# One transformer block with ternary weights: two soft thresholds, summed on TensorE, in place of compare and combine, and new queue orders

## What is computed

```python
def _bitlinear(x, w_latent):
    scale = clip(mean(abs(w_latent), axis=1), 1e-05, None)
    tern = clip(round(w_latent / scale), -1.0, 1.0)
    return x @ (tern * scale).T          # in value
...
h = _bitlinear(x, w_fc) + gate * (x @ v.T @ fast_b.T @ u.T)
r = maximum(h, 0.0)
return _bitlinear(r * r, w_proj)
```

## Time and profile before

| | us |
|---|---|
| median of 3 runs (lowest, highest) | 76.26 (76.23, 77.61) |
| the profiled execution's own time | 76.25 |
| span of its trace | 74.2 |
| busy in the span: PE, DVE, ACT, POOL | 65.0, 52.1, 39.7, 40.2 |

### The profile page before, as it was taken

How to read it: one execution, slowest core, us unless ns; L and a number is a source line. 1 busy time by engine, 2 the same in 40 slices (tenths; PEclk the granted TensorE clock), 3 DMA queues, 4 the chain that set the end, 5 groups by cost and what they waited for, 6 DMA issues and landing times.

```text
span 74.2 us, 2187 instructions
## 1 busy us (share of the span) xinstructions
PE 65.0 (88%) x902; PEld 57.6 (78%) x902; DVE 52.1 (70%) x106; ACT 39.7 (54%) x82; POOL 40.2 (54%) x46
## 2 busy tenths in 40 slices
PE   4999999999999869986678799749999999999950
PEld 3787888889987859974566577449899989999940
DVE  0000049760899999999999999999598344999850
ACT  6100005646794788920059991391739989769000
POOL 7300327891482999999999990000381999800000
PEclk9999999999999999999965559999999999999999
DMA  0999999999300000000000000000000000000044
GB/s 10 297 247 325 372 399 343 390 395 390 117 0 9 0 0 0 4 0 9 9 0 0 0 0 9 0 4 0 9 0 0 0 0 0 9 0 0 0 141 141
DMA packets 3497, 6.74 MB, mean 91 GB/s; under 512 B 528, under 2 KB 1296, under 8 KB 3488
## 3 DMA queue, kind: packets, MB, share of 16 engines
q1 hardware_dynamic: 3488, 6.60, 25.4%
HBM read 6.08 MB, written 0.52 MB: 89 GB/s over the span
## 4 chain that ended last, share of the span: by engine, by line
PE 54%; DVE 39%; issue 3%; ACT 1%
PE psum L312 14%; PE psum L465 10%; PE psum L496 10%; DVE fc_tern L770 7%; PE psum L505 4%; DVE prob_n L856 4%; DVE prob_t L861 3%; PE psum L475 3%; PE psum L414 3%; DVE fc_tern L765 2%; PE psum L407 2%; PE psum L332 2%; DVE k_spread L830 2%; DVE shifted L842 2%; DVE fc_sum L751 2%
## 5 line engine op out<-in xcount | busy, mean ns | idle before, releaser
L602 ACT ACTIVATE std<-mv,eps_sb 128x1 f32<-128x1 f32 x8 | 2.3, 293 | 13.8 <-DVE mv L786 13.8
L1023 POOL TENSOR_TENSOR kqv_sb<-head_sb 128x512 f32<-128x512 f32 x4 | 4.2, 1039 | 10.2 <-ACT head_sb L725 10.2
L782 DVE TENSOR_TENSOR h<-psum,pos_sb 128x256 f32<-128x256 f32 x4 | 1.6, 412 | 9.5 <-PE psum L312 9.5
L725 ACT ACTIVATE head_sb<-psum,fc_scale 128x256 f32<-128x256 f32 x16 | 6.7, 468 | 2.7 <-PE psum L475 2.7
L465 PE MATMUL psum<-zt_hi,fc_t 128*128 128x256 f32 x32 | 8.0, 284 | 0.0
L465 PE MATMUL psum<-zt_lo,fc_t 128*128 128x256 f32 x32 | 7.8, 279 | 0.0
L496 PE MATMUL psum<-sq_hi,mlp_t 128*128 128x256 f32 x32 | 7.8, 282 | 0.0
L496 PE MATMUL psum<-sq_lo,mlp_t 128*128 128x256 f32 x32 | 7.7, 279 | 0.0
L312 PE MATMUL psum<-head_sb 128*128 128x256 f32 x24 | 6.9, 456 | 0.0
L312 PEld LDWEIGHTS psum<-head_sb 128*128 128x128 f32 x24 | 5.5, 239 | 1.3 <-DMA head_sb<-head 0.3
L465 PEld LDWEIGHTS psum<-zt_lo,fc_t 128*128 128x128 f32 x32 | 6.0, 188 | 0.0
(11 more groups left out here) (123 smaller groups left out, 186.5 us busy)
## 6 DMA issues: line engine op xcount, KB each, us to landing
head_sb<-head SPq DMA_DIRECT2D x6, 256.0 KB, 4.9
fc_sb<-w_fc SPq DMA_DIRECT2D x2, 512.0 KB, 7.7
mlp_sb<-w_mlp SPq DMA_DIRECT2D x2, 512.0 KB, 9.1
tail_sb<-tail SPq DMA_DIRECT2D x2, 384.0 KB, 6.4
out_t<-tail_sb SPq DMA_DIRECT2D x4, 128.0 KB, 1.8
pos_sb<-pos SPq DMA_DIRECT2D x1, 256.0 KB, 5.4
kqv_sb<-w_k SPq DMA_DIRECT2D x1, 256.0 KB, 6.5
kqv_sb<-w_q SPq DMA_DIRECT2D x1, 256.0 KB, 6.6
```

Of the source, the lines that this page charges most:

```text
L725: nc.scalar.activation(part[:, a, :], FCB[n][:, a * HT:(a + 1) * HT], ACT.Relu, scale=fc_scale[:, 0, m:m + 1]).then_inc(relu_ready, 1)
L1023: pool.tensor_tensor(sq[:, r, :, :], relu[:, r, :, :], relu[:, r, :, :], ALU.mult).then_inc(sq_pool, 1)
```

## The change

1. **Two soft thresholds in place of compare and combine.** With s the scale, `over` = max(w, s/2) - s/2 and `under` = min(w, -s/2) + s/2 are each made by one instruction from w, independent of each other. PE turns both into the same place in PSUM (one product with the identity starts it, the second adds), and ACT takes the sign while copying out. The unders (8 of fc, 2 of mlp) and the over of the second mlp tile are POOL's, the fc overs DVE's (tiles 0, 1) and ACT's (tiles 2 to 7), the first mlp tile's over is ACT's. PE gets 32 products for fc where there were 16 and 32 for mlp where there were 16; ACT copies all four pieces, now of float32 where they were bfloat16.
2. **All fc sums on DVE**, in two pieces of four tiles.
3. **fast_b is folded into v** (`fold_v`, 2 products) and no longer into u (`fold_u`, 8 products); the transfers of u and v change places with it (u 64 KB late, v 17 KB early).
4. **New queue orders**: on PE `turn(1)` and `value(0)` stand ahead of `scores(0)`; `turn_fc` and `turn_mlp` stand around `project(0)`; `values(1)` and `project(1)` stand behind the first hidden products of half 0, which are split in the product with the rounded part and that with the remainder. `turn(1)` of layer norm 2 stands behind two `mlp_out`. On ACT the rectified tiles of half 1 go one ahead of the squares. Half 0's squares and remainders stay on POOL.

```diff
+        SQ_DVE, SQ_POOL = (4, 5, 6, 7), (0, 1, 2, 3)
...
-            def turn_mlp():
-                pe.wait_ge(mlp_ternary, KE)
...
+            def turn_mlp(i):
+                pe.wait_ge(mlp_over_act, 1)
+                pe.wait_ge(mlp_over_pool, 1)
+                pe.wait_ge(mlp_under_pool, KE)
+                for m in range(4):
+                    h = slice((4 * i + m) * P, (4 * i + m + 1) * P)
+                    for o in range(KE):
+                        c = (m % 2 * KE + o) * P
+                        for n, part in enumerate((mlp_over, mlp_under)):
+                            mm = pe.matmul(mlpt_ps[i][:, m // 2, c:c + P], part[:, o, h], ident_bf[:, :],
+                                           start=n == 0, stop=n == 1)
+                mm.then_inc(mlpt_turned, 1)
...
             turn_fc(0)
             pe.wait_ge(shift_ready, 2)
-            turn_u()
+            turn_fc(1)
             pe.wait_ge(duo_ready, 3)
-            turn_fc(1)
             project(0)
+            turn_mlp(0)
             pe.wait_ge(fct_ready, 1)
-            pe.wait_ge(ut_ready, 2)
-            pe.wait_ge(k_copied, 2)
+            turn_mlp(1)
+            pe.wait_ge(mlpt_ready, 1)
+            turn(0, z, z2t_ps[0], z2_ready, z2t_turned)
+            turn(0, h2, h2t_ps[0], h2_ready, h2t_turned)
+            hidden_main(0, 0, (z2t_hi,))
+            hidden_main(0, 1, (z2t_hi,))
+            low_rank(0)
+            hidden_main(0, 0, (z2t_lo,))
+            hidden_main(0, 1, (z2t_lo,))
+            hidden_low(0, 0)
+            pe.wait_ge(fct_ready, 2)
+            pe.wait_ge(mlpt_ready, 2)
             values(1)
...
+            def fc_signs(i):
+                act.wait_ge(fct_turned, i + 1)
+                nc.scalar.activation(fc_t[:, :, i * 512:(i + 1) * 512], fct_ps[i], ACT.Sign).then_inc(fct_ready, 1)
...
+            fc_signs(0)
             norm_std(0, 1, var2, std2)
+            mlp_signs(0)
             norm_std(1, 1, var2, std2)
+            fc_signs(1)
             copy_out(z2t_hi[0][:, :, :], z2t_ps[0][:, :], z2t_turned, 1, z2t_hi_ready)
-            duo_rows(1)
+            mlp_signs(1)
...
-            def fc_below(tiles):
+            def fc_overs(tiles):
                 dve.wait_ge(fc_scaled, 3)
                 for m in tiles:
-                    dve.tensor_scalar(fc_tern[:, m, :], fc_sb[:, m, :], fc_scale[:, 2, m:m + 1], None,
-                                      ALU.is_lt).then_inc(fc_cmp_dve, 1)
-
-            def ternary(w, scale, tern, m, cmp, count, ready):
-                dve.wait_ge(cmp, count)
-                dve.scalar_tensor_tensor(tern[:, m, :], w[:, m, :], scale[:, 1, m:m + 1], tern[:, m, :],
-                                         ALU.is_gt, ALU.subtract).then_inc(ready, 1)
...
-            def below(w, scale, dst, tiles, scaled, signal):
+            def unders(w, scale, dst, tiles, scaled, signal):
                 pool.wait_ge(scaled, 3)
                 for m in tiles:
-                    pool.tensor_scalar(dst[:, m, :], w[:, m, :], scale[:, 2, m:m + 1], None,
-                                       ALU.is_lt).then_inc(signal, 1)
+                    pool.tensor_scalar(dst[:, m, :], w[:, m, :], scale[:, 2, m:m + 1], scale[:, 1, m:m + 1],
+                                       ALU.min, ALU.add).then_inc(signal, 1)
```

More of the change, by code:

```diff
@@ L463, in hidden_main @@
                     for k in range(KE):
-                        for i, part in enumerate((z2t_hi, z2t_lo)):
-                            pe.matmul(FCB[n][:, a * HT:(a + 1) * HT], fc_t[:, k, m * P:(m + 1) * P],
-                                      part[f][:, k, :], start=a == 0 and k == 0 and i == 0, stop=False,
-                                      skip_group_check=True)
+                        for part in parts:
+                            pe.matmul(FCB[n][:, a * HT:(a + 1) * HT], fc_t[:, k, m * P:(m + 1) * P], part[f][:, k, :],
+                                      start=a == 0 and k == 0 and part is z2t_hi, stop=False, skip_group_check=True)
             def hidden_low(f, j):
@@ L567, in _ @@
+            hidden(0, 2)
+            pe.wait_ge(relu_ready, 2)
+            hidden(0, 3)
             project(1)
-            hidden_low(0, 1)
-            turn_mlp()
-            hidden(0, 2)
+            mlp_out(0, 0)
+            mlp_out(0, 1)
             pe.wait_ge(h2t_ready, 1)
             turn(1, z, z2t_ps[1], z2_ready, z2t_turned)
-            pe.wait_ge(relu_ready, 2)
-            hidden(0, 3)
-            pe.wait_ge(mlpt_ready, 1)
             turn(1, h2, h2t_ps[1], h2_ready, h2t_turned)
-            pe.wait_ge(mlpt_ready_dve, 1)
@@ L578, in _ @@
-            mlp_out(0, 0)
+            hidden_main(1, 0, (z2t_hi,))
             low_rank(1)
-            hidden(1, 0)
-            mlp_out(0, 1)
+            hidden_main(1, 0, (z2t_lo,))
             pe.wait_ge(relu_ready, 6)
-            hidden(1, 1)
+            hidden_main(1, 1)
+            hidden_low(1, 0)
+            hidden_low(1, 1)
             mlp_out(0, 2)
@@ L729, in squares @@
                 act.wait_ge(relu_ready, 2 * n + 2)
-                nc.scalar.activation(sq_hi[:, n % RING, :, :], part, ACT.Square).then_inc(sq_hi_ready, 1)
+                nc.scalar.activation(sq_hi[:, n % RING, :, :], relu[:, n % PART_RING, :, :],
+                                     ACT.Square).then_inc(sq_hi_ready, 1)
             low_high(0)
+            relus(0)
             squares(0)
+            duo_rows(1)
+            relus(1)
+            relus(2)
+            squares(1)
+            squares(2)
             norm_std(2, 1, var2, std2)
             norm_std(3, 1, var2, std2)
-            copy_out(mlp_t[:, 0:4, :], mlpt_ps[0], mlpt_turned, 1, mlpt_ready)
-            squares(1)
+            relus(3)
             copy_out(z2t_hi[1][:, :, :], z2t_ps[1][:, :], z2t_turned, 2, z2t_hi_ready)
-            squares(2)
+            squares(3)
             low_high(1)
-            for n in range(3, HALVES * STEPS):
+            relus(STEPS)
+            for n in range(STEPS, HALVES * STEPS):
+                if n + 1 < HALVES * STEPS:
+                    relus(n + 1)
                 squares(n)
```

306 lines of the change are left out of this document (143 added, 163 removed).

## The result

The changed kernel takes 87.31 us (median of 4 runs, 86.87 to 88.36), the kernel before 76.25 us beside it (76.01 to 77.61). The ratio is 1.144, with a 95% interval of 1.138 to 1.151: slower by 14%, where 72.9 us was forecast. Some executions of one kernel take 1.5% or more longer than its shortest, and this ratio leaves them out (88.36 here, 77.61 before). The profiled execution is the longest of the four, 88.36 us, 1.05 above the median (span 86.4). A second trace of the same kernel, called after_again here, took 88.08.

What follows compares the result with a forecast made beforehand. The middle was taken as bound by DVE, the feed-forward part by PE. Its start moving from 49.31 to 44.3 (-5.0) and length +1.7 gave -3.3, so 76.25 became 72.9 us; range 70.7 to 76.2.

Steps and rivals of the forecast that it cites:

- POOL's price: POOL's eleven threshold instructions: 7.0 us together, 16.4 by the compares' rows; called the unknown.
- I take 0.40: Price assumed for each 256-column threshold on POOL, from the row of two multiplications by constants; the compare's row was 0.940.
- slow POOL: Rival: min and add cost what the compare costs, POOL done at 45.2, PE waits with `turn_mlp`; 78.2 us, chance 0.21.
- The second maximum: Second softmax's maximum on DVE starts at 32.8 instead of 36.64, with two overs replacing eight ternary instructions.
- with unders of 0.94 it is over at 33.5: Condition on `scores(1)`: at 0.40 us per under it ends about 31.9, in time; at 0.94, DVE waits 0.7.
- `project(0)`: PE starts it at 37.1 instead of 41.75, 4.65 us earlier, with `rows_sum(0)` starting at once and taking 0.65.
- 3.5 us behind the maximum's start: End of `duo_rows(0)` on ACT, tied to the second softmax's maximum; moved by 3.84 us, it ends at 36.3.
- The ramp: From `project(0)` to the feed-forward part, decided by ACT's queue: part starts at 42.8 at full clock, taken as 44.3.
- the half level: PE's half clock taken to cover `project(0)`, making what follows 1.45 us later; covering `turn_mlp` too gives 45.2.
- The feed-forward part: PE's last stretch, 1.7 us longer: 22.24 + 0.6 for products moved + 1.1 for waits = 23.9 us.
- Nothing up to the first softmax: Up to 24.8 us the change costs or gains 0, with 0.4 either way.
- no PE wait for the remainders of half 0: PE waiting for `sq_lo` in half 0 was named as a sign that the forecast was wrong.

Runs made afterwards that it cites:

- compare: Changed kernel with POOL's eleven threshold instructions turned into single compares with one pointer (output not the block's): 81.28 us, ratio 1.065.
- cheap: Changed kernel with POOL's eleven threshold instructions turned into two multiplications by 1.0 (output not the block's): 77.52 us, ratio 1.016.
- cheap_hold: As cheap, plus one wait: POOL's low part of square 2 starts only when the second half's z are normalised: 75.62 us, ratio 0.996 to the kernel before.
- hybrid: Kernel before with soft thresholds for fc alone, spread over POOL, DVE and ACT, and small changes of order: 72.90 us, ratio 0.956.
- price list: Kernel before plus eleven forms of POOL's instruction on 128x256 behind the last square, run twice: 93.02 us, which holds the list.
- keys_first: Changed kernel with POOL's two key copies of the second half behind the first lower part of fc instead of the third: 89.93 us, ratio 1.183.
- mlp_off: Changed kernel with the three soft thresholds of the mlp weights moved from POOL to ACT and DVE: 79.12 us, ratio 1.040.

## Why the prediction was wrong

The prediction's layout beside what the profiled executions showed (us; the part's length is from its first product to PE's last end):

| | forecast | after | after_again | compare | cheap | cheap_hold | hybrid | before |
|---|---|---|---|---|---|---|---|---|
| `project(0)` starts | 37.1 | 41.23 | 42.36 | 40.57 | 39.96 | 40.18 | 40.15 | 41.75 |
| `turn_mlp` starts | 40.4 | 50.74 | 50.81 | 45.55 | 41.76 | 41.96 | - | - |
| feed-forward part starts | 44.3 | 56.02 | 56.08 | 49.77 | 45.98 | 46.18 | 46.87 | 49.31 |
| its length | 23.9 | 27.7 | 27.1 | 26.2 | 26.3 | 24.7 | 22.2 | 22.2 |
| time of the execution | 72.9 | 88.36 | 88.08 | 80.82 | 76.91 | 75.61 | 73.84 | 76.25 |

Of the 15.5 us between forecast and profile, 10.3 arise before `turn_mlp` starts, 1.4 between it and the part, 3.8 in the part. Against the median it is 14.4 us.

**POOL's price (10.3 us), the step that failed.** "I take 0.40" was read from the row of two multiplications, and the bounds from that row and the compare's. The prediction held that whether the operation sets the price or the missing second one, "in both the new form is on the cheap side". Neither followed: the rows had no min, and min with add is on the dear side; and a second operation makes a multiplication cheap (0.93 to 0.48), but behind a min it adds 0.3 us. T was 21.9 us, outside the bounds (7.0 to 16.4), so the list was done at 50.64 and not at 35.9: 14.7 us, of which a margin of 4.5 ahead of 40.4 takes the first part. An upper bound must be an upper bound: the compare had one operation, the new form two. With cheap thresholds `turn_mlp` starts at 41.76, so 9.0 of the 10.3 us are the price, and the rest lay under it (the next two paragraphs). The prediction's rival, slow POOL, was the right mechanism with too low a price (PE stands at L442 in front of ready tokens, `std(1)` behind the sign copy, the clock falls with so long a wait). In compare, with nearly its T, `turn_mlp` came at 45.55 for its 45.2; its 78.2 us became 80.82, mostly as the part was 26.2 long.

The prediction weighed the Trainium skill (GPSIMD Engine Reference, section 3.1) on this, by which a body of up to two operations is bound by its port. By that rule bodies this short have one slope. The runs show three: from 256 to 1024 columns it is 0.8 ns a column for mult with mult (0.41 and 1.06 us in cheap), 2.6 for a compare (0.93 and 2.91 in compare), 3.3 for min with add (1.21 in the price list, 3.77 in after). So the rule can hold for mult with mult (0.40 us in the price list), and for no other pair or single tried (0.85 to 1.21).

**The second maximum.** Forecast 32.8; 36.25 after. The condition was named ("with unders of 0.94 it is over at 33.5"); at 1.52 each (4.57 for the three) the key copies were done at 33.4. In cheap, with unders near 0.4, it came at 33.79: the two key copies waited 0.62 us for the second half's keys from ACT, and took 2.24 us, not 1.4.

**`project(0)`.** Forecast 37.1; even cheap had 39.96. The step that tied `duo_rows(0)` to the second maximum ("3.5 us behind the maximum's start") was wrong: it waits for `values(0)`. This stood still for 1.39 us between its 50th product and its 51st, with nothing to wait for that the trace shows, as it had in the kernel before, where DVE's ternary tiles hid it: they kept the second maximum so late that `duo_rows(0)`, behind its exponentials on ACT, was later anyway. So `duo_rows(0)` ended at 38.45 in cheap, 2.15 us behind the forecast's 36.3. And `rows_sum(0)` took 1.33 us instead of 0.65, beside POOL's residual (37.99 to 39.26), and ended 0.55 us behind it, in cheap as in cheap_hold. PE's idle time ahead of `project(0)` is 1.18 us there, from these two.

**The ramp.** From `turn_mlp` to the part 3.9 us were forecast, 4.2 measured in cheap, 5.3 in after at half clock. The forecast's own sum is 0.3 too long here: with `project(0)` at half clock its products end 1.45 us later, but by its own layout the sign had to wait for ACT until 39.9 and not for PE's 39.6, so the part moves by 1.15. The clock itself was misplaced: the half level was put over `project(0)`, which ran at full clock in after, after_again and cheap (1.95 to 1.97 us). In the changed kernel it came behind the two long waits for POOL, in cheap not at all. It is not out of reach there: it covered most of `turn_fc` in compare and its second half in keys_first, and reached into `project(0)` in both (2.38 and 2.74 us).

**The feed-forward part.** Forecast 23.9, measured 27.7. Of the 3.8, 1.6 are the two z behind POOL's subtraction and square (26.3 to 24.7 by one wait); 0.8 remain in cheap_hold as waits mis-sized here; 1.4 are what after has beyond cheap. The two traces, laid over each other from the part's first product, lose all of it in two places, 0.3 up to the remainder of the first hidden tiles (the clock 0.82 from 56 to 58) and 1.1 from the first product of half 1 with `fc_t` to the low-rank products behind it (0.59 and 0.55 from 70 to 74, full in cheap). after_again has only the second of them and is 0.6 shorter. So these 1.4 us go with the half clock; everywhere else the two keep step. The order of the part is a loss by itself: 24.7 us at best, against 22.2 for the old plus 0.6 for what was moved in and out.

**What held.** Nothing up to the first softmax (25.10 for 24.8, within the 0.4 allowed; 25.64 in cheap is outside it); `hidden_factors` done at 27.29 for 27.45; no PE wait for the remainders of half 0; and the idea that the soft thresholds free DVE: hybrid, with its small changes of order, is 3.2 us faster.

## What to carry to other kernels

Moving work to the engine with the most room is only sound with that engine's price for that very form; where no row has it, the upper bound must be built to be one (dearest operation seen, plus a second one), and the work should be cut so that the sum fits at that bound. Split a change into its parts: here the thresholds for fc, spread over three engines and with small changes of order, gave 4.4%, while POOL's list and the new order of the feed-forward part turned that into a loss of 14%. And when the bound of a stretch is taken away, lay out what it was covering, stalls without a releaser too.

## What the runs showed of the hardware

- POOL's tensor_scalar on 128x256: mult with mult 0.40 us, one operation of another kind 0.85 to 0.92, min and add with two pointers 1.21; one multiplication alone is dearer (0.93) than two (0.48 with one pointer). On 128x1024 min and add took 3.77, a compare 2.9, mult with mult 1.05.
- A DVE tensor_scalar of 0.41 us took 1.48 beside a POOL instruction with two tensor inputs, and ended 0.15 us behind it; holding POOL back gave 1.3 us of 76.9 back. Beside a POOL instruction with one tensor input it took 0.41 twice and 1.21 and 1.32 once each. POOL's own instructions stretch too (fc pieces 1.52 us each while DVE worked beside them, 1.20 later).
- `values(0)` stops once in every kernel, with no releaser in the trace: for 1.36 us behind its 46th product before; behind the 50th for 1.39 in cheap, 1.65 in cheap_hold, 1.66 in compare, 1.47 in keys_first, 1.22 in mlp_off, 0.54 in after and 0.87 in after_again; for 1.47 behind the 38th in hybrid, which has `turn_u`'s eight products ahead of it. The place follows the number of instructions, not the time (34.2 to 37.3 us).
- The length of that stop follows a transfer. In these nine traces one 16 KB transfer that the profile files as "instruction" starts 0.7 to 2.0 us before the stop, and PE goes on 1.2 to 1.5 us behind its landing. The two traces of the changed kernel show it best: it takes 0.93 us in after and 1.47 in after_again, it lands at 36.07 and 36.62, and PE goes on at 37.45 and 38.00, 1.38 behind it in both. In these two the 50th product ended 0.84 and 0.51 us behind the landing, in the others from 0.4 us ahead of it to 0.2 behind it; so the stop was short. That PE waits for its instructions fits all of this; no run was made to try it.
